# A pipelined decoder layer: three matmuls woven together, and four pieces of a recurrence step moved in their queues

## The reference

```python
xxx = x + xx * time_maa_x                                  # xx: x shifted by one token, less x
a = jnp.tanh(xxx @ time_maa_w1).reshape(B, T, 5, D)        # D = 32
m = jnp.einsum('btfd,fdc->fbtc', a, time_maa_w2)           # five mixes: w, k, v, r, g
xw = x + xx * (time_maa_w + mw)                            # and xk, xv, xr, xg alike
r, k, v = xr @ W_r.T, xk @ W_k.T, xv @ W_v.T
g = jax.nn.silu(xg @ W_g.T)
w = time_decay + jnp.tanh(xw @ time_decay_w1) @ time_decay_w2
def step(S, inp):                                          # 8 heads of 64, 128 tokens
    r_t, k_t, v_t, d_t = inp                               # d = exp(-exp(w))
    kv = k_t[..., :, None] * v_t[..., None, :]
    y = jnp.einsum('bhj,bhji->bhi', r_t, S + u[None, :, :, None] * kv)
    return (d_t[..., None] * S + kv, y)
```

## Time and profile before

| | |
|---|---|
| Time of the kernel, median of 3 runs (lowest to highest) | 881.57 us (880.63 to 882.44) |
| Span of the profiled execution | 888.4 us |
| PE busy in it | 840.1 us, 95% |
| DVE busy in it | 740.6 us, 83% |
| ACT busy in it | 505.2 us, 57% |
| POOL busy in it | 138.5 us, 16% |
| Mean granted PE clock | 0.975 |

### The profile page before, as it was taken

How to read it: one execution, slowest core, us unless ns; L and a number is a source line. 1 busy time by engine, 2 the same in 40 slices (tenths; PEclk the granted TensorE clock), 3 DMA queues, 4 the chain that set the end, 5 groups by cost and what they waited for, 6 DMA issues and landing times.

```text
span 888.4 us, 23836 instructions
## 1 busy us (share of the span) xinstructions
PE 840.1 (95%) x10134; PEld 678.1 (76%) x10134; DVE 740.6 (83%) x1206; ACT 505.2 (57%) x728; POOL 138.5 (16%) x197
## 2 busy tenths in 40 slices
PE   7898999999999999998989899999999988999997
PEld 6798888888888888887877788888888854444453
DVE  5977989899898989977475598889889889999995
ACT  4566373756637274651623344445535457999995
POOL 1001010100202010010102000000000123577441
PEclk9899999999999999998979999999999989999999
DMA  8330103030121202024040322320331230243311
GB/s 268 108 108 20 43 17 106 14 99 24 41 70 34 88 14 84 15 71 159 24 168 1 129 85 96 143 103 39 142 142 45 88 96 26 72 140 110 108 60 60
DMA packets 36552, 72.41 MB, mean 82 GB/s; under 512 B 6080, under 2 KB 6976, under 8 KB 35432
## 3 DMA queue, kind: packets, MB, share of 16 engines
q1 hardware_dynamic: 35912, 68.93, 23.5%
q0 software_dynamic: 544, 2.10, 0.6%
HBM read 58.39 MB, written 12.58 MB: 80 GB/s over the span
## 4 chain that ended last, share of the span: by engine, by line
PE 76%; DVE 14%; issue 4%; POOL 4%; ACT 1%; DMA 0%; DVEq 0%; POOLq 0%; ACTq 0%
PE P L62 11%; PE P L64 9%; PE P L63 9%; PE S L734 6%; PE S L2270 5%; PE P L2256 5%; POOL sm L376 3%; DVE E L1842 2%; PE S L628 2%; PE P L649 2%; PE S L62 2%; PE S L1703 2%; PE S L64 2%; PE S L63 2%; PE S L1690 2%
## 5 line engine op out<-in xcount | busy, mean ns | idle before, releaser
L376 POOL TENSOR_TENSOR sm<-sm,mhalf 128x16 f32<-128x16 f32 x8 | 30.6, 3828 | 315.7 <-DVE sm L1103 315.7
L734 PE MATMUL S<-R,K 64*64 64x32 f32 x3072 | 59.3, 225 | 5.8 <-DVE K L1054 3.9
L734 PEld LDWEIGHTS S<-R,K 64*64 64x64 f32 x3072 | 53.4, 140 | 12.7 <-issue 7.4
L2270 PE MATMUL S<-wq,hqT 128*128 128x512 bf16 x256 | 60.2, 380 | 2.4 <-ACT hqT L2194 2.0
L2256 PE MATMUL P<-wq,xqT 128*128 128x512 bf16 x256 | 59.8, 388 | 1.0 <-ACT xqT L2172 1.0
L1008 DVE TENSOR_TENSOR xf<-P,xx 128x1024 f32<-128x1024 f32 x40 | 48.8, 1220 | 11.8 <-PE P L649 11.7
L1842 DVE TENSOR_SCALAR E<-S,upper 128x2048 f32<-128x2048 f32 x16 | 37.6, 2349 | 24.2 <-PE S L1690 24.0
L1516 ACT ACTIVATE E<-E 128x2048 f32<-128x2048 f32 x16 | 30.6, 1914 | 47.0 <-DVE E L1842 47.0
L1848 DVE RECIPROCAL rec<-S 128x512 f32<-128x512 f32 x16 | 53.6, 3351 | 1.9 <-PE S L1705 1.9
L1015 DVE TENSOR_TENSOR xf<-xf,xnT 128x1024 f32<-128x1024 f32 x40 | 49.1, 1227 | 1.1
L1051 DVE TENSOR_TENSOR R<-R,D 128x256 f32<-128x256 f32 x96 | 40.5, 422 | 10.7 <-PE S L734 10.3
(11 more groups left out here) (300 smaller groups left out, 2706.7 us busy)
## 6 DMA issues: line engine op xcount, KB each, us to landing
wch<-in_wff SPq DMA_DIRECT2D x32, 256.0 KB, 3.1
cwch<-in_wff SPq DMA_DIRECT2D x8, 1024.0 KB, 6.5
xt<-in_x SPq DMA_DIRECT2D x8, 512.0 KB, 4.6
y<-in_x SPq DMA_DIRECT2D x8, 512.0 KB, 3.6
out<-y SPq DMA_DIRECT2D x8, 512.0 KB, 3.3
cxt<-out SPq DMA_DIRECT2D x8, 512.0 KB, 4.2
ct<-in_ctx SPq DMA_DIRECT2D x8, 512.0 KB, 5.0
cxr<-out SPq DMA_DIRECT2D x8, 512.0 KB, 6.6
```

The source lines that it names most:

```text
L376: pool.tensor_tensor(sm[:, 2, :], sm[:, 1, :], mhalf[:, 0:2 * H], ALU.pow).then_inc(y_rstd, 1)
L734: mm = pe.matmul(ps[half_rows(side), par, b, k, :], K[head_rows(par), r % 2, at:at + HALF], right_tokens(par, g, side, i), start=True, sto ...
L2270: mm = pe.matmul(O[:, :], hqT[b % 2][:, k, :], w2q[:, k, :], start=k == 0, stop=k == NF - 1)
```

## The change

1. `values(1)` issues its matmuls in threes (across of its own half, within the second half, within the first), as `values(0)` did; before it issued 16 `within` and then 8 `across` matmuls.
2. In steps with both `p` and `r` the narrow product moves on PE from before level 5 to between levels 5 and 6. ACT's code for its tanh becomes a function of its own at the same place.
3. On DVE the factors of level 0 come first in a step; `shift` follows level 0, and `lo(q, 4)` follows level 1.
4. The bonus product on PE moves from before level 2 to before level 3, and writes its corner in X2 instead of L. DVE's `place_bonus` moves from before the factors of level 5 to behind them, and behind the first of the four instructions of `lower_stack`.
5. On ACT one of the three later copies into `stack` moves between `accept_wide` of level 5 and of level 6.

No instruction is added or taken away.

```diff
-    dg = L[:, 2 * C - HALF // 2:2 * C - HALF // 2 + 2 * H]
+    dg = X2[:, 2 * C - HALF // 2:2 * C - HALF // 2 + 2 * H]
...
             if t_:
                 accept_wide(r, 5)
                 if last_levels(q, r):
                     x["bias_q"](0)
+                if f:
+                    stack_second(p, 1, 2)
                 accept_wide(r, 6)
             if f:
-                stack_second(p)
+                stack_second(p, 2 if t_ else 1, 4)
                 stack_last(p)
...
                 else:
+                    across_rows(1, h, False, h == H - 1)
                     within_rows(0, 1, h, False, h == H - 1)
                 mm = within_rows(part, 0, h, h == 0, h == H - 1)
-            if part == 1:
-                for h in range(H):
-                    mm = across_rows(1, h, False, h == H - 1)
             return mm
...
             if t_:
-                pe.wait_ge(A_part, 5 * r + 1)
-                for b in range(2):
-                    mm = pe.matmul(dg.rearrange("p (a b k) -> p b a k", a=2, b=2)[:, b, :, :], turned_bonus[:, T * b:T * b + T],
-                                   ident[:, :].rearrange("p (k m) -> p m k", m=XD)[:, 0:2, :], start=True, stop=True)
-                mm.then_inc(bonus_done, 1)
                 level(r, 2)
...
             if t_:
+                pe.wait_ge(A_part, 5 * r + 2)
+                for b in range(2):
+                    mm = pe.matmul(dg.rearrange("p (a b k) -> p b a k", a=2, b=2)[:, b, :, :], turned_bonus[:, T * b:T * b + T],
+                                   ident[:, :].rearrange("p (k m) -> p m k", m=XD)[:, 0:2, :], start=True, stop=True)
+                mm.then_inc(bonus_done, 1)
                 level(r, 3)
...
             if t_:
                 level(r, 5)
+            if t_ and f:
+                narrow(p, q)
             if last:
                 x["q_chunk"](0, 3)
...
-            if s_:
+            if s_ and not t_:
                 lo(q, 4)
-            if f:
-                shift(p)
             if t_:
                 if r == 0:
                     dve.wait_ge(zeroed, 2)
                 level(r, 0)
+            if f:
+                shift(p)
...
             if t_:
                 level(r, 1)
+            if s_ and t_:
+                lo(q, 4)
...
                 level(r, 4)
+                level(r, 5)
+            if f:
+                lower_stack(p, 0, 1)
+            if t_:
                 place_bonus(r)
-                level(r, 5)
-            if f:
-                lower_stack(p)
+            if f:
+                lower_stack(p, 1, 4)
```

More of the change, by code:

```diff
@@ L428, in stack_first, with narrow_tanh @@
                 stack_rows(j, 0)
+        def narrow_tanh(p):
             act.wait_ge(a1_done, p + 1)
@@ L432, in stack_first, with stack_second @@
                                X0[D_MIX * quarter:D_MIX * quarter + D_MIX, C:C + HALF], ACT.Tanh).then_inc(a_tanh, 1)
-        def stack_second(p):
-            for j in range(1, 4):
+        def stack_second(p, j0, j1):
+            for j in range(j0, j1):
                 stack_rows(j, 2 * D_MIX)
@@ L512, in step @@
                 stack_first(p)
+                narrow_tanh(p)
             if t_:
@@ L650, in mix, with narrow @@
             mm.then_inc(m_done, 1)
+        def narrow(p, q):
+            if q is not None:
+                pe.wait_ge(k_ready, q + 1)
+            for k in range(NC):
+                for quarter in range(4):
+                    mm = pe.matmul(X0[D_MIX * quarter:D_MIX * quarter + D_MIX, C:C + HALF], w1[:, k, 4 * D_MIX:5 * D_MIX],
+                                   xf[0][:, k, HALF * quarter:HALF * quarter + HALF], start=k == 0, stop=k == NC - 1)
+            mm.then_inc(a1_done, 1)
         def channel_major(n, ps, m):
@@ L832, in step @@
                 mm.then_inc(a_done, 1)
-                if s_:
[L834 to L839, removed]
+                if not t_:
+                    narrow(p, q)
             if q == 0:
@@ L1083, in rk, with lower_stack @@
             dve.tensor_tensor(PY[:, :, :].rearrange("p k t -> p (k t)"), X1[:, :], K[:, q % 2, :], ALU.mult).then_inc(rk_ready, 1)
-        def lower_stack(p):
-            for j in range(4):
+        def lower_stack(p, j0, j1):
+            for j in range(j0, j1):
                 dve.wait_ge(stacked, 8 * p + (1, 3, 4, 5)[j])
@@ L1173, in step @@
                 level(r, 4)
-                place_bonus(r)
                 level(r, 5)
             if f:
-                lower_stack(p)
+                lower_stack(p, 0, 1)
+            if t_:
+                place_bonus(r)
+            if f:
+                lower_stack(p, 1, 4)
             if f:
```

## The result

The changed kernel is **slower by 0.71%**: over 9 executions of each its median is 890.66 us (887.42 to 893.47) against 882.44 us (880.63 to 889.91), ratio 1.0071, 95% interval 1.0046 to 1.0097. Measured again later on another chip the ratio was 1.009 (1.0064 to 1.0115). The prediction said 882.8 us, and its range ended at 886.0.

The account below looks back on a forecast made before the run. PE was 95% busy, but PE and DVE were taken to hand the path to each other. Terms of -0.5, -0.7, +0.4 and +2.0 summed to +1.2 us on the 888.4 us span, less 6.8: 882.8 us, range 879.4 to 886.0.

Parts of the forecast that it names:

- 0.1 us per steady step: Steps 4 to 8: net gain after PE's savings and DVE's longer chain; five such steps, -0.5 us.
- PE loses 0.47 us at level 3: Steady step: DVE's level 2 factors come 1.07 us later, so the second half of PE's level 3 waits 0.47 us.
- The chain from level 5 to the first mix: DVE, steady step: factors 1.47, low parts 1.75, bonus 1.35, some 0.1 overlap; first mix at 316.57 instead of 316.39.
- sum of +1.2: Whole kernel: -0.5 - 0.7 + 0.4 + 2.0 = +1.2 us on a span of 888.4 us.
- Step 3: Factors first remove DVE's wait, xrl gives most back; with 0.59 for the narrow product, -0.7 us.
- values(1) in threes: PE's second value product takes 1.09 us instead of 1.83, 0.74 less; DVE's third mix can use 0.28 per steady step.
- Step 9 and 10: Bonus behind level 5 delays ACT's acceptances and the value product: +0.4 us in step 9, +2.0 us net in step 10.
- Rival E: The threes save nothing in values(1): +0.74 in step 10, about 0.3 per steady step; +3.6, 885.2 us. Chance 0.06.
- rival B: Clock falls behind step 10's wait of about 2.5 us before values(0): +2 us or more, 885. Chance 0.27.
- gives nothing: Step 9: the shorter values(1) lies beside ACT's work and gains no time.
- 6.8 us from span to median: Base: median without profiler, 881.57, lies 6.8 us below the 888.4 us span; difference carried over unchanged.
- Rival C: Step 10's half-clock stretch is shorter; two of three q pieces at full clock give -2.6, 879.0 us. Chance 0.15.

Follow-up runs that it names:

- second execution of before: The kernel before, once more, with no edit, for a second profile: span 880.0, ratio to before 0.9995 (0.9974 to 1.0015).

## Why the prediction was wrong

**The net of a steady step, "0.1 us per steady step" to the good, is the step that failed first.** It was 0.31 us to the bad. Three sizes add up to the difference of 0.4; the mechanisms of a steady step were those of the prediction.
- *The step that stood for all was not typical.* The distance from level 0 to the v product was 324.42 - 294.87 = 29.55 us there, and 272.81 - 243.40 = 29.41 in the one before, like the others (29.38 to 29.41). 0.14 us of a chance delay counted as room.
- *"PE loses 0.47 us at level 3"* was 0.57 against the same step: from level 0 to level 3's second half both agree with the working (the last factor ends 9.80 us behind level 0 as worked out), but PE's next product comes 0.1 us later behind a second half that waited. (The working's own numbers give 313.12 - 313.0 = 0.12 for the hand-over that it calls 0.15, which changes the sum by 0.03.)
- *The chain from level 5 to the first mix* was taken as 4.48 us with some overlap, and is 367.84 - 363.20 = 4.64. The low part, the bonus and the three low parts stand 0.03 us apart instead of overlapping by 0.08.

The head alone costs 0.81 us a step and the bonus 0.39 where the head is as before, while threes and narrow product gain 0.79 together. In the changed kernel head and bonus partly lie over each other. The prediction had every one of the four, and found them to cancel; the misses of a few tenths of a microsecond are paid in every steady step. Five times 0.41 us is 2 of the 5 us by which the sum of +1.2 missed the 6 us that the changed kernel lost at one clock; step 3, next, is another 0.7.

**Step 3** was to gain 0.7 us. The distance between the v products there is 50.27 us against 50.23 in the second execution of before: nothing. The working left the bonus out of step 3 and gave the head almost nothing. The traces have 50.27 in the changed kernel, 49.81 with the head as before and 49.42 with the bonus as before too: the head costs 0.46 us there and the bonus 0.39. Level 4 starts 12.28 us behind level 0 instead of 12.20, and takes 1.41 us instead of 1.14, so it waits within.

**values(1) in threes:** 1.09 us, right, and so was the 0.28 us that a steady step can use. In step 10, between the two turns of y, traces with 3.4 us at half clock have 49.0 to 49.2 us with the threes and 49.7 to 49.9 without, which fits the 0.74. Rival E, that the threes save nothing, is refuted. The rule quoted for it from the Trainium skill, "TensorE: Matmul & The Clock Gate", section "The mechanism", that loads on the same rows do not pass, does not describe what these alternating tiles do: the same two in three share rows in both value products, and both take 1.09 us.

**Step 9 and 10.** In step 10 the mechanism was right: PE waits 2.51 us for the 2.5 predicted, and the bonus product at half clock took 457.77 - 456.99 = 0.78 us for 0.8. (The shift of the value product is 475.5 - 473.69 = 1.8 by the working's own numbers, and not 1.9.) In step 9 the wait was 1.42 us, where the working has 421.3 - 420.96 = 0.3. It took PE's arrival from a trace in which PE ran at half clock for 6.8 us of that step and came late; in the changed kernel's first trace it did not. The price of the bonus in both steps, 0.4 + 0.8 + 1.9 = 3.1 us, fits the 3.2 to 4.2 that taking it back gave at one clock, each good to about 1 us.

The clock, rival B, had a part in the measured times, but not in the way B had it. B's fall behind values(0) of step 10 is in the first trace (0.50 granted at 472.66 to 476.07), yet filling that wait brought no time. The kernel with the higher clock was the one filled in step 9, behind the shorter values(1), a place that the prediction had called "gives nothing". By itself the longer wait there (2.32 us instead of 1.56) is only what the shorter values(1) left over; what the threes lost is the clock, 0.980 instead of 0.984 or some 2.8 us. The Trainium skill, "TensorE: Matmul & The Clock Gate", section "What's actually happening", quoted for B, says that activity releases the throttled state. Both filled traces agree in so far as the clock is 1.00 behind the filled wait; the mean clock was higher with the filling in step 9 alone.

**The base.** Carrying 6.8 us from span to median took the profiled execution for a usual one. Rival C, a shorter stretch at half clock, was in the second execution of before: 3.4 us in step 10 instead of 13.7. Chance in the one trace was taken for the kernel's habit; besides, the nine executions beside the changed kernel have a median of 882.44, 0.9 above the three of the prediction.

What stays open: at one clock the changed kernel loses 6 us, and the traced pieces (5 x 0.31 for the steady steps, nothing in step 3, 3.2 to 4.2 for the tail, less 0.7 for the threes in step 10) give 4 to 5; the rest has no place yet. Why some kernels have a lower mean clock than others is open too: it varies between executions of one kernel by more than between the kernels (0.971 to 0.987 for the changed kernel). A kernel with the bonus' product early and its copy late was not tried, since PE would then write the area while DVE reads the corner.

## What to carry to other kernels

Before an instruction is moved to fill a wait, look at what the engine does with the time that it leaves: factors that come first must wait for their input, and the idle microsecond is paid by whatever was put behind them. Here the factors of level 0 came first, DVE stood for 1.08 us, and PE waited for DVE at level 3. Where four moves each of half a microsecond are summed, take the reference from several equal steps and not from one, and price hand-overs from rows where the reader really waited. Time saved on the busiest engine is worth only what the next engine can follow, and the clock can take back what the steps gained: compare times of kernels only beside their mean granted clocks. And a filling of a wait should be shorter than the wait.

## What the runs showed of the hardware

- Over 120 executions of one kernel a mean granted clock that was lower by 0.001 went with 0.6 us more time (of 884).
- With 14 idle products (3.3 us) put into a wait of 2.3 us in step 9 the mean granted clock was 0.985 and not 0.980 (threes), and 0.983 and not 0.980 (threes and narrow). The same filling in a wait of 2.5 us in step 10 left it at 0.983.
- Of two executions of the same kernel one had a granted clock of 0.88 from 400 to 500 us and the other 0.97, and their spans differ by 8.4 us.
- 48 instructions on 64 x 64 tiles took 1.09 us when three tiles alternated, and 1.83 us as 32 on two tiles and 16 on one. In both, one group started 0.06 us after the group before it, whether it held three, two or one.
